# Fourteen of sixteen sums of absolute FFN weights go from the graph build into the experts

## The reference

```
x = x + layernorm(x) @ W0.T + bias            # W0: 1024 x 1024, built from 41250 edges (scatter-add)
x = x + moe(layernorm(x))                     # 8 experts, top 2, capacity 314, 1024 -> 512 -> 1024
x = x + gcn(layernorm(x), edges, W, b)        # neighbours' sum with degree norms
x = x + bitlinear(gelu(bitlinear(layernorm(x), w1)), w2)
bitlinear(x, w) = quant_act(x) @ quant_weight(w).T
quant_weight(w): s = max(mean(|w|), 1e-5); clip(round(w / s), -1, 1) * s
```

## Time and profile before

| | us |
|---|---|
| median of 3 runs (1058.28 to 1063.33) | 1059.43 |
| the profiled execution: time | 1062.41 |
| its span, first to last instruction | 1060.7 |
| mean granted PE clock | 0.976 |
| PE's first work of layer 0 | 136.66 |
| PE busy / DVE busy / ACT busy | 980.4 / 737.7 / 464.2 |
| chain that ended last, shares: PE, DVE, issue, DMA, ACT | 75%, 13%, 6%, 3%, 2% |

### The profile page before, as it was taken

One profiled execution on the slowest core, in us unless ns is written; L12 is line 12 of the kernel. 1 busy time (PEld: TensorE's weight loads), 2 busy tenths in 40 slices (PEclk: granted clock), 3 DMA queues, 4 the chain that ended last, 5 costly groups with the idle time before them and its releaser, 6 DMA issues.

```text
span 1060.7 us, 17400 instructions
## 1 busy us (share of the span) xinstructions
PE 980.4 (92%) x6781; PEld 535.5 (50%) x6781; DVE 737.7 (70%) x1037; ACT 464.2 (44%) x573; POOL 127.8 (12%) x139
## 2 busy tenths in 40 slices
PE   0799889997899999999979999899999999999997
PEld 0688645553555666665534444444444444444443
DVE  7999778786755556668679754999977555555440
ACT  5488645651444554445532113999733111222221
POOL 6300034230211111000043100011000000000000
PEclk9898899999799999999989999999999999999999
DMA  3757525553677777673556855789413545544430
GB/s 118 243 199 256 183 80 199 199 219 113 249 244 275 258 259 263 257 249 119 166 161 179 217 125 180 284 317 309 173 40 70 129 114 115 118 110 110 110 77 35
DMA packets 166031, 188.90 MB, mean 178 GB/s; under 512 B 126505, under 2 KB 126827, under 8 KB 161871
## 3 DMA queue, kind: packets, MB, share of 16 engines
q1 hardware_dynamic: 159567, 165.47, 49.4%
q0 software_dynamic: 6400, 22.55, 6.9%
HBM read 137.98 MB, written 35.33 MB: 163 GB/s over the span
## 4 chain that ended last, share of the span: by engine, by line
PE 75%; DVE 13%; issue 6%; DMA 3%; ACT 2%; DVEq 0%; SPq 0%; POOL 0%; ACTq 0%; POOLq 0%
PE ps L1090 20%; PE ps L1318 13%; PE ps L1289 13%; PE ps L1200 9%; PE ps L1216 6%; DVE fq L2258 3%; PE ps L1271 2%; PE ps L1157 2%; DMA eo_d<-eo 2%; PE ps L1023 2%; DVE w1l L2095 2%; DVE stats L1757 1%; PE ps L977 1%; PE ps L950 1%; DMA abs_in<-in_L_ffn_w 1%
## 5 line engine op out<-in xcount | busy, mean ns | idle before, releaser
L1318 PE MATMUL ps<-w2q,hqt 128*128 128x512 fp8e4 x640 | 140.8, 379 | 1.4 <-DVE out_t L2361 1.4
L1289 PE MATMUL ps<-w1q,xqt 128*128 128x512 fp8e4 x640 | 139.9, 379 | 0.6 <-issue 0.6
L1638 ACT ACTIVATE hf<-ps,fs 128x512 f32<-128x512 f32 x80 | 54.9, 687 | 183.2 <-PE ps L1289 183.2
L2342 DVE TENSOR_REDUCE hm<-hf 128x1 f32<-128x512 f32 x80 | 54.2, 685 | 73.9 <-ACT hf L1638 73.9
L1289 PEld LDWEIGHTS ps<-w1q,xqt 128*128 128x128 f16 x640 | 62.4, 98 | 75.9 <-issue 1.1
L1318 PEld LDWEIGHTS ps<-w2q,hqt 128*128 128x128 f16 x640 | 62.3, 98 | 75.7 <-DVE out_t L2361 1.9
L1090 PE MATMUL ps<-gwt_h,xt 128*128 128x512 f16 x320 | 84.5, 379 | 0.9 <-issue 0.9
L1090 PE MATMUL ps<-wt_h,xt 128*128 128x512 f16 x320 | 85.3, 379 | 0.0
L1200 PE MATMUL ps<-xdh,w1h 128*128 128x314 f16 x256 | 76.3, 298 | 2.8 <-DVE w1l L2095 2.7
L1200 PE MATMUL ps<-xdh,w1l 128*128 128x314 f16 x256 | 75.8, 296 | 0.0
L1200 PE MATMUL ps<-xdl,w1h 128*128 128x314 f16 x256 | 75.6, 295 | 0.0
(11 more groups left out here) (315 smaller groups left out, 1907.7 us busy)
## 6 DMA issues: line engine op xcount, KB each, us to landing
abs_in<-in_L_ffn_w SPq DMA_DIRECT2D x32, 1024.0 KB, 5.7
wstage<-in_L_ffn_w SPq DMA_DIRECT2D x32, 1024.0 KB, 10.7
fnat_b<-in_L_ffn_w SPq DMA_DIRECT2D x28, 512.0 KB, 6.0
fnat_a<-in_L_ffn_w SPq DMA_DIRECT2D x27, 512.0 KB, 5.2
eo_d<-eo SPq DMA_DIRECT2D x16, 512.0 KB, 3.0
hq_d<-hq SPq DMA_DIRECT2D x8, 1024.0 KB, 6.3
xs_d<-xs_all SPq DMA_DIRECT2D x10, 512.0 KB, 2.9
bias_b<-in_L_ffn_w SPq DMA_DIRECT2D x9, 512.0 KB, 5.3
```

What stands on the lines that cost most here:

```text
L1289: last = mm(ps[:, n % 4, :], xqt[:, u, k, :], w1q[:, k // 2, n * 512:(n + 1) * 512, k % 2], start=(k == 0), stop=(k == KD - 1))
L1318: last = mm(ps[:, 4 + h, :], hqt[:, u, k, :], w2q[:, k // 2, h * 512:(h + 1) * 512, k % 2], start=(k == 0), stop=(k == KF - 1))
L1638: cp(hf[:, i % 2, n * 512:(n + 1) * 512], ps[:, n % 4, :], ACT.Gelu, scale=fs[:, i % 2, 3:4]).then_inc(s_ge, 1)
L2342: last = v.tensor_reduce(hm[:, u, n:n + 1], hf[:, u, n * 512:(n + 1) * 512], AX.X, ALU.max, apply_absolute_value=True)
```

## The change

Sixteen pieces of w1 were summed in the build. Now two of them are summed in layer 0 as its 17th and 18th sum (at its ninth tile), and the 14 others in experts 0 to 6, two in each, from one new buffer `abs_e` of 1 MB. The DVE reduction, the PE matmul and the thresholds are computed in the last expert. SP's loop over the pieces in the build is gone, so that it goes on at once to b1c and to layer 0's first pieces.

```diff
@@ sync
-            sp.wait_ge(s_rows, 1)
-            with sp.Fori(0, sp.value_load(rounds_i[0:1, 0:1], min_val=1, max_val=FINAL)) as r:
-                for m in range(16):
-                    sp.wait_ge(s_absr, 16 * r + m + 1)
-                    sp.dma_start(abs_in[:, m % 2, :], f1_pieces[m]).then_inc(s_absinr[m % 2], 16)
-                sp.wait_ge(s_absr, 16 * r + 18)
-                hold(sp)
+            f1_rest = f1_in.rearrange("a b -> (a b)")[2 * P * 2048:].rearrange("(e j p c) -> e j p c", j=2, p=P, c=2048)
...
-                if i < KD:
+                if i <= KD:
                     for u in range(2):
                         sp.wait_ge(s_abs, 2 * i + u + 1)
-                        sp.dma_start(abs_in[:, u, :], f2_pieces[2 * i + u]).then_inc(s_absin[u], 16)
+                        sp.dma_start(abs_in[:, u, :], f2_pieces[2 * i + u] if i < KD else f1_pieces[u]).then_inc(s_absin[u], 16)
...
+            def abs_rows(e, j):
+                sp.wait_ge(s_absr, 2 * e + j + 1)
+                sp.dma_start(abs_e[:, :], f1_rest[e, j]).then_inc(s_absinr, 16)
...
                 else:
+                    abs_rows(e, 0)
                     for q in range(4):
                         sp.wait_ge(s_wl, 4 * e + q + 1)
                         expert_piece(e + 1, q)
...
                         sp.dma_start(expert_rows[e][s * P:s * P + SM[s], :], eo[0:SM[s], u, :]).then_inc(s_eout[u], 16)
+                        if s == 1 and not last_of(e, NE):
+                            abs_rows(e, 1)
@@ tensor
-            pe.wait_ge(s_swp, 1)
-            mm(ps[:, 3, 16:18], ones32[:, :], sw[:, 0:2], start=True, stop=True).then_inc(s_swm, 1)
...
                             if s == 0 and h == 0:
+                                pe.wait_ge(s_swp, 1)
+                                mm(ps[:, 3, 32:34], ones32[:, :], sw[:, 0:2], start=True, stop=True).then_inc(s_swm, 1)
                                 ranks()
@@ scalar
-                    if 6 <= b < 22:
-                        abs_round(r, b - 6)
...
+            def abs_rows(e, j):
+                act.wait_ge(s_absinr, 16 * (2 * e + j) + 16)
+                hold(act)
+                cp(abs_e[:, :], abs_e[:, :], ACT.Abs, accum_out=abs_acc[:, bass.ds(2 * e + j + 2, 1)]).then_inc(s_absr, 1)
...
                     for q in range(2):
                         split_high(e + 1, q)
+                    abs_rows(e, 0)
                     act.wait_ge(s_g2, 1 + 6 * e + 6)
                     for q in range(2, 4):
                         split_high(e + 1, q)
+                    abs_rows(e, 1)
@@ vector: line 2075 to 2076 and lines 2223 to 2227 go
             def ranks():
+                dve.wait_ge(s_swm, 1)
+                do(v.tensor_scalar(sw[:, 2:4], ps[:, 3, 32:34], 1.0 / (D * FH), Q_EPS, ALU.mult, ALU.max))
+                v.tensor_scalar(sw[:, 4:6], sw[:, 2:4], 0.5, None, ALU.mult).then_inc(s_swh, 1)
+                dve.wait_ge(s_swh, 1)
+                do(v.tensor_scalar(sw[:, 6:8], sw[:, 2:4], -0.5, None, ALU.mult))
...
             def last_expert(e, ep):
+                dve.wait_ge(s_abs, 2 + 18)
+                dve.wait_ge(s_absr, 1 + 2 * (NE - 1))
+                v.tensor_reduce(sw[:, 0:2], abs_acc[:, :].rearrange("p (m n) -> p m n", m=2), AX.X, ALU.add).then_inc(s_swp, 1)
                 w1_low(0)
```

More of the change, by code:

```diff
@@ L238, in build_kernel @@
         ht32 = sb("big", "ht32", [P, 2, CAP], F32)
+        abs_e = sb("big", "abs_e", [P, 2048], F32)
         cur["route"] = OFF_BIG + 49152
@@ L373, in build_kernel @@
         s_absr = sem("s_absr")
-        s_absinr = [sem(f"s_absinr{u}") for u in range(2)]
+        s_absinr = sem("s_absinr")
         s_abs = sem("s_abs")
@@ L1343, in _ @@
             act.sem_inc(s_bev, 2)
-            act.sem_inc(s_absr, 2)
+            act.sem_inc(s_absr, 1)
             act.sem_inc(s_abs, 2)
@@ L1389, in batch @@
                 done.then_inc(s_bev, 1)
-            def abs_round(r, m):
-                act.wait_ge(s_absinr[m % 2], 128 * r + 16 * (m // 2) + 16)
-                cp(abs_in[:, m % 2, :], abs_in[:, m % 2, :], ACT.Abs, accum_out=abs_acc[:, m:m + 1]).then_inc(s_absr, 1)
+            def abs_rows(e, j):
+                act.wait_ge(s_absinr, 16 * (2 * e + j) + 16)
+                hold(act)
+                cp(abs_e[:, :], abs_e[:, :], ACT.Abs, accum_out=abs_acc[:, bass.ds(2 * e + j + 2, 1)]).then_inc(s_absr, 1)
             def abs_piece(m, u):
@@ L1399, in abs_piece @@
                 hold(act)
-                cp(abs_in[:, u, :], abs_in[:, u, :], ACT.Abs, accum_out=abs_acc[:, bass.ds(16 + m, 1)]).then_inc(s_abs, 1)
+                cp(abs_in[:, u, :], abs_in[:, u, :], ACT.Abs, accum_out=abs_acc[:, (16 + m) % 32:(16 + m) % 32 + 1]).then_inc(s_abs, 1)
             def counts(r, t, part):
@@ L2074, in _ @@
             v.tensor_copy(tok_i[:, :], ps[:, 2, 0:3 * NE]).then_inc(s_toki, 1)
-            dve.wait_ge(s_abs, 2 + 16)
-            v.tensor_reduce(sw[:, 0:2], abs_acc[:, :].rearrange("p (m n) -> p m n", m=2), AX.X, ALU.add).then_inc(s_swp, 1)
             dve.wait_ge(s_ex, 1)
@@ L2221, in _ @@
             dve.wait_ge(s_dinv2, 2)
-            dve.wait_ge(s_swm, 1)
-            do(v.tensor_scalar(sw[:, 2:4], ps[:, 3, 16:18], 1.0 / (D * FH), Q_EPS, ALU.mult, ALU.max))
-            v.tensor_scalar(sw[:, 4:6], sw[:, 2:4], 0.5, None, ALU.mult).then_inc(s_swh, 1)
-            dve.wait_ge(s_swh, 1)
-            do(v.tensor_scalar(sw[:, 6:8], sw[:, 2:4], -0.5, None, ALU.mult))
             pairs(dve, expert, NE)
```

## The result

The changed kernel takes 1057.38 us (median of 20 runs, 1054.58 to 1063.7) beside 1060.92 us of the kernel before on the same chip: ratio 0.9966, 95% interval 0.9955 to 0.9978. It gains about 3.5 us where 6.8 were forecast, and the time lies 4.8 us over the forecast one; the other 1.5 us of that are the start of the sum, a median of three runs (1059.43) that lay under the one of 20 (1060.92).

What follows compares the result with a forecast made beforehand. PE was taken as busy for most of the span, so gains come only where something else holds it up: -7.5 - 0.5 + 1.0 + 0.2 = -6.8 us, from 1059.43 to 1052.6 us; range 1048 to 1060.

Steps and rivals of the forecast that it cites:

- the build's sum of 7.5 us: Graph build without its 16 sums: four gains added up to 7.5 us, between 4.4 and 9.7.
- term A: Build: the 14.00 us tile interval, where ACT's sum delayed a copy, falls to the clean 10.44, gaining 3.56 us.
- The experts' term: Experts 0 to 6: sum 0 free in ACT's hole, sum 1 delaying PE 0.15 us each, 1.0 us in all.
- B: Build: the 11.28 us tile interval likewise falls to the clean 10.44, gaining 0.84 us.
- C: End of build, last tile with weights: DVE's 2.12 us of idling for ACT's copy is gained.
- D: After the build's last gap: PE's low clock and slow narrow products avoided, 0 to 3.2 us, taken as 1.0.
- rival 2: Build: the clock falls all the same, 2.1 us of the first interval's gain and the clock gain lost; net -3.7, 1055.7; chance 0.18.
- Startup: Start of the experts: the threshold matmul's 0.58 us wait leaves the chain, gain 0 to 0.58, taken as 0.5.
- Rival 1: Experts: sum 1's data lands late, PE loses 0.9 us each, 6.5 in seven; net -1.3, 1058.1 us; chance 0.14.
- rival 4: Experts: sum 1 lands after 7.6 us, PE loses 1.7 us in each of seven; slower, 1063.6 us; chance 0.06.
- Last expert: Last expert: the reduction on DVE behind the maxima adds some 0.2 us.
- covered: Last expert: the three threshold operations, about 0.6 us ahead of the ranks, hidden because DVE soon idles 1.28 us for ACT.

Runs made afterwards that it cites:

- second profile: The changed kernel run again with no edit; 1058.41 us, ratio 0.9957 to the kernel before.
- the kernel with one load: Changed kernel with its 14 sums in the experts fed by only the first load, 13 loads left out; 1056.24 us (0.9951), again 1055.73 (0.9941).
- the build's half: Changed kernel without the 14 loads and sums in the experts, one threshold made from the other's sums; 1055.74 us (0.9928), again 1056.01 (0.9947).
- the later sum: Changed kernel with one sum moved behind the next expert's second hth copy, the other's load behind the weight pieces; 1056.75 us (0.9954), again 1056.05 (0.9952).
- fourth profile: The changed kernel with no edit, run beside the later sum on one chip; 1057.86 us, ratio 0.9955 to the kernel before.
- the experts' half alone: Kernel before, all 16 sums still in the build, plus 14 unused loads and sums in experts 0 to 6; 1063.66 us, ratio 1.0002.

## Why the prediction was wrong

The direction was right, and so were the places where the build gives and the experts take. The step that failed is the build's sum of 7.5 us, above all its term A: 3.56 us were counted, the builds give 1.9. The experts' term was too small as well, 1.0 for about 1.8. Of the 4.8 us between forecast and time, 3.3 are the gain, and 1.5 are the median of three runs from which the sum was taken.

**Build, forecast -7.5, measured about -5.2.** Between the two profiles that the forecast was tied to, the build shrank by 6.9 us (136.66 to 129.72). But four builds with their loads end at 136.66, 134.20, 134.79 and 133.79, mean 134.9; those of the five profiles of the changed kernel at 129.72, 128.97, 131.02, 129.69 and 128.99, mean 129.7. The first profile was the slowest of the four. The forecast even noted that its execution took 3 us more than the median, read its terms from it, and then subtracted them from the median: part of that execution's bad luck was counted as gain.

- A (3.56): the interval of 14.00 is 12.65, 12.38 and 12.74 in the other builds with loads, and 10.6 to 11.5 in those of after. It never comes down to the clean 10.44. The step "limited by DVE's one-hot work" was said of the other intervals; it holds of this one too, where DVE has no idle time left. From the means of the four and of the five: 1.9 us.
- B (0.84): 11.28 to 10.44, as forecast. The other builds with loads had 11.18, 11.14 and 10.44 there; by the means it is 0.6 us.
- C and D (2.12 and 1.0): the interval that held C and the narrow products of D was 13.02 (113.98 to 127.00) and is 8.88 (111.08 to 119.96), so the pair shows 4.1 us. In the other builds with loads it was 11.43, 12.28 and 10.43; by the means it is 2.7 us. What D counted came back: the 16 narrow products take 1.90 us again (117.61), and the clock is 0.99 from 125 to 130 us. But the clock is low elsewhere, 0.74 from 107 to 112 and 0.69 from 120 to 125 us. So rival 2 was right that it falls all the same, and wrong that A gives back only PE's own gap and D nothing. That its 3.7 us are close to the measured gain is chance. Why the clock is low there stays open.

**Startup, forecast -0.5, measured about -0.2.** To the fillers it is 17.85 to 17.87 us with the thresholds at the start and 17.31 to 17.33 without, in all 18 profiles: 0.55, as forecast. But most of it is lost again in the fillers, which run at a granted clock of 0.50 at first (268 to 272 us of after, 275.4 to 279 of before) and take 5.2 to 6.4 us with the thresholds there and 5.0 to 6.7 without. From layer 0's last products to the first expert it is 29.7 us on average with (four profiles) and 29.5 without (fourteen), single ones 28.6 to 30.1. The forecast followed the wait and not what stood behind it.

**Experts, forecast +1.0, measured about +1.8.** Rival 1's mechanism, in some experts and not in all. The working was close: 0.69 us in hand were forecast, and waits of ACT of 1.06 and 1.14 (second profile) and 2.82 us (fourth) made periods longer by 0.50, 0.60 and 2.25, so about 0.55 were. The landing was not one number. ACT's waits in the seven experts were 0.4 to 1.3 us in the first profile, with one of 2.82 in the fourth, when the load took 7.58 us: rival 4's landing, once. The five profiles lose 0.3, 1.9, 2.2, 2.9 and 1.7 us. The first was the luckiest, as before's was the unluckiest. By time, the kernel with one load is 3.1 us faster in the one set that had both. The 0.15 an expert was taken from single loads of the build, where no store stood just ahead.

The Trainium skill ("DMA: Bandwidth & Descriptors", Latency and other measured facts) was quoted for a higher latency at high load. The slices of the profile's page have 297 to 345 GB/s in the experts. The loads of abs_e took 5.3 us in the median there, less than the 5.7 of the earlier trace rows, and 7.58 in the one read above; the twelve that before's build issued between 60 and 110 us had all landed in 4.7 to 5.6. So the trace agrees for single loads and not for the typical one: the spread grew.

**Last expert, +0.2, and what was counted at nothing.** Sums 17 and 18 stand in ACT's hole of layer 0 (its idle time before the rows' copy at 246.41 is 6.39 us instead of 10.18), and layer 0 is no longer for them (120.7 to 121.0 us from its first to its last products in the five profiles, 120.7 in the two of before). The reduction takes 0.18 us. But "covered" was wrong of the thresholds' 0.6 us: up to its last product of w2 the last expert takes 31.14 or 31.15 us in the four profiles with the thresholds at the start, and at least 31.88 in all others, that with only the thresholds moved among them. PE's wait of 1.39 us for the relu costs nothing beside that: the changed kernel's first profile has 31.91 with it, the kernel with one load 31.90 without. From the last expert's start to the end of the program it is 571.2 us in both profiles of before, 571.3 with only the thresholds moved, and 570.0 to 572.5 in the five of the changed kernel, mean 571.4. So 0.2 is about right for the whole, within that scatter and by another way than forecast; what gives the rest of the 0.75 back is not known.

Put together by stretches: -5.2 - 0.2 + 1.8 + 0.2 = -3.4 us, against differences of the medians of 3.5 to 5.0 us in four sets and about 3 in the fifth (the five ratios: 3.7 us on average). The six runs whose experts lose nothing (the build's half, one load, the later sum, two of each) gain 5.8 us on average of their ratios, 2.1 more than the changed kernel. That is the experts' loss by time.

**What would show it.** "No tile interval over 10.6": wrong (11.46). "Layer 0's first PE work at about 129": 129.72, right. "A period of 28.9 to 29.1": right in the first profile, over it in the other four. "ACT's idle before sum 1 under 0.7 us": 0.39 to 0.76 in six experts of the first profile, 1.30 in the seventh. "No wait of PE for ACT": wrong in all five, 0.75 to 2.00 us in the last expert, and 2.09 in another one of the fourth profile.

## What to carry to other kernels

Sizes read from one execution belong to that execution: where its own time lies off the median, take the same interval from two or three profiles before subtracting it from the median, and take the median itself from more than three runs. Follow a wait that goes to the next fixed point behind it: 0.55 us were gained ahead of the fillers, and most of them were lost in the fillers. A load with one buffer and a consumer 5 us behind its issue costs by its late landings, so price it by the spread; the cure here was to move the consumer (every period was whole again), not the issue (no gain). Before moving work forward on an engine, look who is queued behind the results that it delays: sum 0 one step earlier cost 1.6 us an expert through two other engines.

## What the runs showed of the hardware

- An engine's own work in idle time can be free even when it nearly fills that time. With ACT at 53.90 of 60 us the build ended at 129.98, within the 128.70 to 131.02 of the builds without sums (by time up to 1.4 us stay open), and 4.2 us more of ACT an expert changed neither the periods nor, in the set that had both kernels, the time by more than 0.3 us. The loads that fed that work did.
- PE's granted clock was 0.74 from 107 to 112 us of after, a mix of its levels of 1.2 and 2.4 GHz, though PE's only gaps from 88 us on had been of 0.58 and 0.19 us. After a gap of 2.27 us in an expert it was 0.61 for 4.4 us (the experts' half alone, from 410.6), and after one of 2.09 us at the same place it stayed at 1.00 (the changed kernel's fourth profile, from 317.9).
- From the tile that starts at about 60 us to its end, the build takes 72.9 to 76.6 us with its loads (four profiles) and 68.8 to 70.0 without (fourteen): the loads make it longer and three times as uneven. The changed kernel's seven experts vary by 2.6 us, while without the loads, or with the later sum, each period repeats to 0.04 us.
